# A cross-attention stage: a mask product moves to ScalarE, small row factors to GpSimd, and one of two TensorE turns of q becomes a transposing transfer

## What is computed

```python
q = layernorm(x).reshape(b, l, 16, 16)
k = v = ctx.reshape(b, l, 16, 16)
scores = einsum('bqhd,bkhd->bhqk', q, k)
scores = where(mask == 0, -1e20, scores)
attn = softmax(scores / 16, axis=3)
out = einsum('bhqk,bkhd->bqhd', attn, v).reshape(b, l, e)
x = x + out @ W_out.T + b_out
```

## Time and profile before

| | us |
|---|---|
| median of 3 runs | 1359.58 (1357.98 to 1359.6) |
| the profiled execution, its own time | 1363.24 |
| its span, first to last instruction | 1361.4 |
| attention stage in the span | 0 to about 350 |

### The profile page before, as it was taken

One profiled execution on the slowest core, in us unless ns is written; L12 is line 12 of the kernel. 1 busy time (PEld: TensorE's weight loads), 2 busy tenths in 40 slices (PEclk: granted clock), 3 DMA queues, 4 the chain that ended last, 5 costly groups with the idle time before them and its releaser, 6 DMA issues. The chain is left out here.

```text
span 1361.4 us, 28305 instructions
## 1 busy us (share of the span) xinstructions
PE 1171.8 (86%) x10148; PEld 891.0 (65%) x10148; DVE 886.5 (65%) x2626; ACT 586.8 (43%) x1033; POOL 574.7 (42%) x604
## 2 busy tenths in 40 slices
PE   0689999999377989978769999939999999999996
PEld 0144444444223658866659888827998999999995
DVE  4999999999687641237365685515666666556663
ACT  1377777776444723234056423303333333333331
POOL 4577777774250019975000006551333333333333
PEclk9999999999598999989879999969999999999999
DMA  9477777774310025520488033237888888888781
GB/s 279 78 168 159 165 167 169 159 153 141 126 62 1 1 93 170 181 112 0 125 202 180 1 124 115 91 105 246 248 248 256 257 251 244 253 254 247 240 255 59
DMA packets 183548, 217.29 MB, mean 160 GB/s; under 512 B 92944, under 2 KB 166288, under 8 KB 170912
## 3 DMA queue, kind: packets, MB, share of 16 engines
q1 hardware_dynamic: 169152, 199.19, 50.8%
q0 software_dynamic: 14304, 16.93, 5.9%
HBM read 144.70 MB, written 52.23 MB: 145 GB/s over the span
## 5 line engine op out<-in xcount | busy, mean ns | idle before, releaser
L1977 PE MATMUL banks<-moe_w,moe_hT 128*128 128x256 f16 x2640 | 296.9, 273 | 0.0
L1977 PEld LDWEIGHTS banks<-moe_w,moe_hT 128*128 128x128 f16 x2640 | 258.3, 98 | 30.0
L1888 ACT ACTIVATE moe_hf<-banks,moe_b 128x256 f32<-128x256 f32 x440 | 184.9, 471 | 170.1 <-PE banks L1964 170.1
L1832 POOL DMA_INDIRECT out_x<-moe_y,slot_owner x78 | 121.7, 1561 | 285.6 <-DVE moe_y L2210 249.8
L1964 PE MATMUL banks<-moe_rT,moe_w 128*128 128x256 f16 x1872 | 212.5, 274 | 0.0
L703 DVE CUSTOM_DVE_ANT_0 masked<-banks,mask_bias 128x256 f32<-128x256 f32 x512 | 185.4, 417 | 22.8 <-PE banks L511 22.6
L1964 PEld LDWEIGHTS banks<-moe_rT,moe_w 128*128 128x128 f16 x1872 | 184.1, 98 | 21.6
L442 ACT ACTIVATE probsT<-banks 128x1024 f32<-128x1024 f32 x128 | 131.0, 1024 | 69.9 <-PE banks L542 69.8
L2097 DVE TENSOR_TENSOR moe_hT<-moe_hf,moe_hT 128x512 f16<-128x512 f32 x220 | 153.4, 697 | 7.6
L511 PE MATMUL banks<-kT,qT 48*128 48x256 f16 x512 | 92.6, 286 | 61.0 <-DMA qT<-q_split 30.3
L1818 POOL DMA_INDIRECT slots_x<-moe_xn,pos x64 | 64.1, 1001 | 158.7 <-DVE pos L2161 122.9
(11 more groups left out here) (310 smaller groups left out, 1796.3 us busy)
## 6 DMA issues: line engine op xcount, KB each, us to landing
moe_w<-moe_halves SPq DMA_DIRECT2D x80, 1024.0 KB, 5.0
moe_halves<-half_parts SPq DMA_DIRECT2D x18, 1024.0 KB, 6.2
slots_x<-empty_row SPq DMA_DIRECT2D x1, 10140.0 KB, 51.5
moe_rows<-slots_x SPq DMA_DIRECT2D x39, 260.0 KB, 5.9
half_rows<-in_L_ffn_Wfc SPq DMA_DIRECT2D x8, 1024.0 KB, 8.7
half_rows<-in_L_ffn_Wproj SPq DMA_DIRECT2D x8, 1024.0 KB, 8.0
moe_b<-in_L_ffn_bproj SPq DMA_DIRECT2D x39, 128.0 KB, 5.4
ctx_rows<-in_ctx SPq DMA_DIRECT2D x16, 256.0 KB, 3.1
```

The costliest lines, as they stand in the source:

```text
L1832: pool.indirect_dma_start(out=out_rows, out_offset=bass.IndirectOffsetOnAxis(ap=owner[:, s, t:t + 1], axis=0), in_=y[s % 2][:, t, :], in_o ...
L1888: ins = act.activation(hf[p][:, j, :], src, ACT.Gelu_apprx_tanh, bias=b1[buffer][:, j:j + 1], scale=1.0 / WSCALE)
L1977: ins = pe.matmul(OUT[p][:, t * D:(t + 1) * D], hT[p][:, x, j, t * P:(t + 1) * P], w2[buffer][:, w, j, :], start=(j == 0 and (w, x) == PAR ...
```

## The change

Three edits. `set_live` goes from DVE at hp 0 to POOL, at the start of the phase. `set_mask` goes from DVE at hp 3 to ACT at hp 4, as activations with a scale for each row. Half 1 of q with its maxima is no longer turned by PE and copied by ACT: a new step `turn_max(B)` at the head of SP's phase issues two transposing transfers into the second half of `qmT`. `split_q(B+2)`, which overwrites what they read, now waits for them. The rest is semaphore counts.

```diff
@@ SP
+            def turn_max(b):
+                sp.wait_ge(s_mp, 4 * b + 4)
+                if b >= 1:
+                    sp.wait_ge(s_qm, 32 * b)
+                if b >= 2:
+                    sp.wait_ge(s_ST, HP * (b - 1))
+                for t in range(NQ):
+                    sp.dma_start_transpose(qmT[b % 2][:, HP // 2:, t * P:(t + 1) * P],
+                                           q_split[b % 2][:, t, HP:, :, :].rearrange("p h a e -> p (h a e)")).then_inc(s_qm, 16)
...
             for B in PHASES:
+                if real(B):
+                    turn_max(B)
                 if real(B + 1):
                     turn_mask(B + 1)
@@ POOL, split_q(b)
                 if b >= 2:
-                    pool.wait_ge(s_rT, 2 * (b - 1))
+                    pool.wait_ge(s_rT, b - 1)
+                    pool.wait_ge(s_qm, 32 * (b - 1))
...
+            def set_live(b):
+                s = b % 2
+                T = NQ * b
+                group = 0 if b == 0 else 1 if b < 4 else 2
+                pool.wait_ge(s_ml, 2 * b + 2)
+                if b >= 2:
+                    pool.wait_ge(s_mb, b - 1)
+                pool.tensor_scalar(row_live[s][:], row_top[s][:], 0.0, None, ALU.is_equal).then_inc(s_rl, 1)
+                pool.wait_ge(s_rl, b + 1)
+                pool.wait_ge(s_ln, ln_steps(group, 1))
+                if b >= 2:
+                    pool.wait_ge(s_qn, b - 1)
+                pool.tensor_tensor(live_scale[s][:], rstd[:, T:T + NQ], row_live[s][:], ALU.mult)
+                pool.tensor_tensor(live_shift[s][:], nmr[:, T:T + NQ], row_live[s][:], ALU.mult).then_inc(s_lv, 1)
...
             for B in PHASES:
+                if real(B + 2):
+                    set_live(B + 2)
                 if B >= -1:
                     cut_piece(pool, g.cut, 2 * (B + 1))
@@ ACT
+            def set_mask(b):
+                s = b % 2
+                act.wait_ge(s_lv, b + 1)
+                if b >= 2:
+                    act.wait_ge(s_mT, 32 * (b - 1))
+                    act.wait_ge(s_red, 2 * HP * (b - 1))
+                for t in range(NQ):
+                    ins = act.activation(mask_bias[s][:, t, :], mask_all[s][:, t, :], ACT.Copy, scale=row_live[s][:, t:t + 1])
+                ins.then_inc(s_mb, 1)
...
-                    if hp == 0 and real(B):
-                        copy_max(B, 1)
                     if hp == 6 and real(B + 1):
-                        copy_max(B + 1, 0)
+                        copy_max(B + 1)
...
+                    if hp == 4 and real(B + 2):
+                        set_mask(B + 2)
@@ PE, scoresT(b, hp, j, k)
                 if hp % (HP // 2) == 0 and (j, k) == (1, 0):
-                    pe.wait_ge(s_r, 2 * b + hp // (HP // 2) + 1)
+                    if hp == 0:
+                        pe.wait_ge(s_r, b + 1)
+                    else:
+                        pe.wait_ge(s_qm, 32 * (b + 1))
...
-                    if hp == 0 and real(B):
-                        if real(B - 1):
-                            pe.wait_ge(s_ov, 4 * B - 1)
-                        max_back(B, 1)
@@ DVE
-                    if hp == 0 and real(B + 2):
-                        set_live(B + 2)
...
-                    if hp == 3 and real(B + 2):
-                        set_mask(B + 2)
```

More of the change, by code:

```diff
@@ L223, in attention @@
         s_mb = sem("mask_bias_ready")
+        s_rl = sem("row_live_ready")
         s_lv = sem("live_scale_ready")
@@ L227, in attention @@
         s_qT = sem("q_transposed")
+        s_qm = sem("q_max_transposed_by_transfer")
         s_rT = sem("q_max_in_psum")
@@ L278, in load_mask @@
                 if b >= 2:
-                    sp.wait_ge(s_ml, 3 * (b - 2) + 1)
+                    sp.wait_ge(s_ml, 2 * (b - 2) + 1)
                 sp.dma_start(mask_int[b % 2][:], mask_view[:, b, :, :]).then_inc(s_mask[b % 2], 16)
@@ L442, in exponent, with copy_max @@
                 act.activation(probsT[n % EXPS][:].rearrange("p j k q -> p (j k q)"), psum_t[n % 2][:], ACT.Exp, scale=SCALE).then_inc(s_exp, 1)
-            def copy_max(b, half):
-                act.wait_ge(s_rT, 2 * b + half + 1)
-                if half == 0 and b >= 2:
+            def copy_max(b):
+                act.wait_ge(s_rT, b + 1)
+                if b >= 2:
                     act.wait_ge(s_ST, HP * (b - 1))
                 src = psum_o.bitcast(F16).rearrange("p (h q) -> p h q", h=HP // 2)
-                act.activation(qmT[b % 2][:, half * HP // 2:(half + 1) * HP // 2, :], src, ACT.Copy).then_inc(s_r, 1)
+                act.activation(qmT[b % 2][:, 0:HP // 2, :], src, ACT.Copy).then_inc(s_r, 1)
             def copy_out(b, quad):
@@ L490, in _, with max_back @@
             pe.wait_ge(s_set, 6)
[L492 to L495, removed]
+            def max_back(b):
+                pe.wait_ge(s_mp, 4 * b + 2)
+                for hp in range(HP // 2):
                     for t in range(NQ):
-                        at = (i * NQ + t) * P
+                        at = (hp * NQ + t) * P
                         ins = pe.transpose(psum_o.bitcast(F16)[:, at:at + P],
@@ L602, in _ @@
                     if hp == 1 and real(B - 1):
-                        if real(B):
-                            pe.wait_ge(s_r, 2 * B + 2)
                         weigh(B - 1, 3)
@@ L618, in _ @@
                             pe.wait_ge(s_ov, 4 * B + 2)
-                        max_back(B + 1, 0)
+                        max_back(B + 1)
                     if hp == 6 and real(B - 1):
@@ L623, in _ @@
                         if real(B + 1):
-                            pe.wait_ge(s_r, 2 * (B + 1) + 1)
+                            pe.wait_ge(s_r, B + 2)
                         weigh(B, 2)
@@ L669, in see_mask @@
                 v.wait_ge(s_mask[s], 16 * (b // 2 + 1))
+                if b >= 2:
+                    v.wait_ge(s_mb, b - 1)
                 v.tensor_scalar(mask_all[s][:], mask_int[s][:], 0, MASKED, ALU.is_equal, ALU.mult).then_inc(s_ml, 1)
@@ L673, in see_rows_live @@
                 s = b % 2
-                v.wait_ge(s_ml, 3 * b + 1)
+                v.wait_ge(s_ml, 2 * b + 1)
+                if b >= 2:
+                    v.wait_ge(s_rl, b - 1)
                 v.tensor_reduce(row_top[s][:], mask_all[s][:], AX.X, ALU.max).then_inc(s_ml, 1)
[L677 to L694, removed]
             def take_max(b, hp, j):
```

## The result

| | before | after |
|---|---|---|
| median, us | 1359.49 (4 runs, 1357.98 to 1359.6) | 1374.09 (4 runs, 1371.09 to 1380.99) |
| ratio | | 1.0115, 95% interval 1.0082 to 1.0149 |
| the profiled execution, its own time | 1363.24 | 1373.51 |
| last `add` of the attention begins at | 349.49 | 364.47 |

What follows compares the result with a forecast made beforehand. DVE paced an ordinary phase, PE close behind, but the loop's 1.3 us of slack was expected to decide. Terms: -5.9 us by Q(13), +3.4 in phase 14, -0.9 in phase 15, together -3.4, giving 1356; range 1340 to 1369.

Steps and rivals of the forecast that it cites:

- case A: In the attention, the loop paces intervals at 18.8 us after halves and 16.6 otherwise: median 1356; chance 0.55.
- the loop: On SP and POOL, `turn_q` through context load, `split_k`, `values`, `split_q` to next `turn_q`: 16.57 us without PE and ACT waits.
- rival C: In the six intervals after halves the turn lands late, 20.9 us instead of 18.8: median 1369; chance 0.25.
- the sign named for it: Intervals between `turn_q` starts after halves over 19.8 us would show the forecast wrong.
- the price of `turn_max` after halves: In SP's queue behind the 2 MB of weight transfers, it makes the interval after an odd phase 18.8 us.
- The landing, "9.7 later" than `load_half`: After odd phases the turns of the maxima land with the end of the burst, 9.7 us after `load_half`.
- PE's stall at hp 4 after halves lies mostly beside the loop: In even phases PE stalls 4.0 us for the maxima, making a later phase 1 us late, without growing.
- Phase 14, "3.4 lost": Behind queued FFN weights the maxima land at Q(13) + 20.7; phase 15 begins at + 29.1 instead of + 25.7.
- The start: In phases -1 and 0 DVE loses 1.8 us and ACT 0.9, so the first `turn_q` comes at 60.5.
- DVE's share of a phase: In an ordinary phase DVE loses 2.2 us of mask and live-row steps, leaving 15.1 us of work.
- the odd phases 3 to 11: A phase bound only by PE and DVE was put at 16.2 us, from 15.4 to 17.
- `set_mask` on ACT: Two tiles of 128x256 take ACT 0.8 to 1.1 us a phase, costed at nothing; without cover 1 us.

Runs made afterwards that it cites:

- experiment 13: The change, with PE multiplying the identity 52, 64 and 64 times where it would stand in phases 4, 10 and 14: 1380.86 us, ratio 1.0075 to before.
- 1: Kernel before with only `set_live` on POOL and `set_mask` on ACT, half 1 of q still turned by PE: 1346.85 us, ratio 0.9904.
- 2: Kernel before with only `turn_max` added, mask and live steps staying on DVE: 1365.28 us, ratio 1.0045.
- experiment 4: Kernel before with both engine steps moved, maxima turned on PE, and `load_ctx` issued ahead of `turn_q`: 1344.9 us, ratio 0.9891.
- 12: The kernel of experiment 4 with the expert weights' transfers beside the attention cut to a few columns: attention's last `add` begins at 336.4 us.
- 9: The change with expert-weight transfers cut to a few columns and FFN weights behind the last `turn_max`: attention's last `add` at 336.9 us instead of 364.5.
- 10: Kernel before with the expert weights' transfers cut to a few columns: attention's last `add` at 351.5 us, against 349.5 for before.
- 3: The change with `store_half`, `load_half` and the FFN weights issued behind the next phase's `turn_max`: 1359.95 us, ratio 1.0006 to before.
- 6: The change with `store_half` and `load_half` issued from ACT's queue at hp 7 of odd phases, FFN weights behind the last `turn_max`: 1369.31 us, ratio 1.0074.
- 5: The change with weight transfers issued behind the next phase's `turn_max` and `load_ctx` ahead of `turn_q`: 1367.75 us, ratio 1.0056 to before.

## Why the prediction was wrong

**What failed.** The prediction chose between its case A (the loop holds, 1356) and its rival C (the turns land late after halves, 1369), to which it gave 0.25. C's mechanism is the larger part of what happened, and the sign named for it came: intervals after halves over 19.8. That the median lies inside C's spread of 1362 to 1375 is partly luck: with the 20.1 measured C's six intervals give +4, about 1364, and the rest came of things that neither case held. The step that failed is the price of `turn_max` after halves, in three terms.

1. *The landing, "9.7 later" than `load_half`.* Measured for the second turn: 12.0 in phase 4, and 13.4 in phase 10 (`load_half` issued at 235.45, second turn 239.2 + 9.7 = 248.9). I read it off one small mask turn and took the two turns as a pair that lands with the burst's end. In fact each issue takes longer beside the burst (6.12 us for both instead of 2.5), so the second goes out 3.3 us after the first, and it then needs up to 10 us of its own. With it the interval behind odd phases became 20.1 instead of 18.8: six times 1.3 is 8 us of the 14.3 by which the middle was off.

2. *"PE's stall at hp 4 after halves lies mostly beside the loop."* It doesn't. I had the maxima at Q + 16.0 and the next phase at Q + 24.7; in phase 3 to 4 they landed at 136.6, which is Q + 19.0, and phase 5 began at 148.2, Q + 30.6. `split_max` ends a phase, `turn_max` waits for it, and in SP's queue the mask, k and q turns stand behind `turn_max`: a late phase pulls the next `turn_q` with it. Q(5) and Q(11) come 9.7 and 9.2 us after the start of their phases, near the 7.7 that the issues alone take. Half of the 5.9 us by which phase 5 is late is the landing; the other half is a term that the prediction put at nothing: behind the stall the clock is at the lower level, and the rest of the phase takes 11.6 us instead of the 8.7 it reckoned (8.9 to 9.2 at full clock, experiment 13). Late phases made the other intervals 17.5 instead of 16.6, the other 6 us; this reading is from the trace. Experiments 1 and 2 bear it out: 18 us of the loss come only when both parts are there, next to 21 us more of PE's wait and 28 us more of low clock.

3. *Phase 14, "3.4 lost".* The maxima landed at 327.3, which is Q(13) + 22.0 and not + 20.7, and the rest of the phase took 10.0 at a fallen clock and not 8.4. Phase 15 began at Q(13) + 32.0, so 6.3 were lost.

The start was off too: Q(0) came at 62.0, 1.5 later than the 60.5 forecast. So Q(13) was 305.3 - 289.5 = 15.8 late, and the 2.9 of phase 14 bring that to the end, 18 us later than forecast.

**What held.** DVE's share of a phase is 15.3 (15.1 forecast), and the odd phases 3 to 11 take 16.0 to 16.7 (16.2). `set_mask` on ACT takes 0.90 for two tiles (0.8 to 1.1) at no cost that shows. `set_live` on POOL took 0.6 (0.5):

```profile
128.25 0.22 POOL L425 TENSOR_SCALAR row_live<-row_top 128x2 f32<-128x2 f32 x1
128.55 0.20 POOL L430 TENSOR_TENSOR live_scale<-rstd,row_live 128x2 f32<-128x2 f32 x1
128.70 0.20 POOL L431 TENSOR_TENSOR live_shift<-nmr,row_live 128x2 f32<-128x2 f32 x1
```

In quiet phases the turns land 2.4 after each issue, so no cost there. The Trainium skill's figure (VectorE: DVE Perf Modes, The three transpose paths; 1309 ns a tile by DMA) would make that an estimate of 5.2 us for the four tiles of an issue; the trace disagrees. The same page's advice (Rules for kernel authors), TensorE where PSUM will do, holds here for a reason that the figure doesn't give: with the turn on PE the end hardly depends on what else is being transferred (336.7 with the burst, 336.4 without, experiments 4 and 12).

**What is shown, what is argued.** Shown: the engine steps gain, the transfer loses (1, 2); the loss hangs on the burst (9, 10) that is under way when the turn is issued (3), also from another queue (6). Argued from traces only: that SP's row of issues, drawn out by the burst, is the next limit (5), and that a late phase delays the next `turn_q`. Open: how the loss divides between POOL's wait, PE's wait and PE's fallen clock. That the transfer beside the burst loses against before doesn't hang on it.

The better kernel is experiment 4, both engine steps with the maxima turned on PE and the context earlier: 1344.9, 1.1% below before; with the steps alone it is 1346.85, and the two can't be told apart by their times.

## What to carry to other kernels

Before a step goes from an engine to a transfer, look at what the transfer engines carry in the microseconds when it will be issued, and price it by its worst landing there, for the last of its issues and not the first; a queue of another engine gave little of it back here (1.0074 instead of 1.0115). If a buffer is read within a phase of being sent, a stall there delays the step that issues the next such transfer, so it need not stay beside the loop. Time each part of a change by itself: here a gain of 1% lay under a larger loss.

## What was unexpected of the hardware

- The length of a stall of PE doesn't tell whether its granted clock falls. In the change's trace it was at the lower level, 1.2 GHz, for 7 to 10 us around the ends of the stalls of 4.9, 6.5 and 6.4 us, for 3.6 us after one of 1.6, and for 3.6 us from 74.6 on with no idle time over 0.8 us just before; after stalls of 1.2, 1.3, 2.1 and 3.8 (the last ends at 55.6) it stayed up. In the second trace of the same kernel it fell with stalls of 3.4, 4.9 and 7.5 us and after one of 1.7, and not after two of 2.2. At the lower level the x16 matmuls of `weigh` took 1.93 instead of 1.07 us.
- A transposing issue of 1.2 us grows to 3.2 while 2 MB of other transfers drain, also when these come from another engine's queue, and its landing from 2.4 to between 6 and 10 us.
- Three operations of GpSimd on two elements a row took 0.2 us each, against the 0.99 of the earlier trace rows.
